# Two long VectorE instructions of a hybrid-block kernel, each in two parts with a recurrence update between

## The chip, the cores and the metric

The kernel runs on one core of one Trainium2 chip. The metric is the device time of one execution in microseconds (us), as the median of the runs. A core has TensorE (PE, with its weight loads as PEld), VectorE (DVE), ScalarE (ACT), GpSimd (POOL) and SyncE (SP, which issues DMAs here). Each works through its own queue of instructions in order; semaphores are all that ties one queue to another.

## The reference

The input x is 8 sequences of 1024 tokens with 256 features. Four layers follow each other, each added to its normalised input: a gated linear attention with its own feed-forward part, a mixture of experts, a recurrence, and the mixture of experts again.

```python
x = x + attn_a(layernorm(x))     # gated linear attention, then h + gelu(ln(h) @ W1 + b1) @ W2 + b2
x = x + ffn(layernorm(x))        # 8 experts, top 2 by softmax of x @ router_w.T
x = x + attn_b(layernorm(x))     # h_t = tanh(x_t @ B + h_(t-1) @ A.T), then hs @ C @ W_out.T + b_out
x = x + ffn(layernorm(x))
```

The recurrence is serial over all 1024 tokens: every step needs the state of the step before. The attention is computed in chunks of 32 tokens: scores of a chunk are multiplied by a causal mask, and a state is carried from chunk to chunk.

## The kernel before, in words

The 1024 tokens are cut into 32 blocks of 32 tokens; a block holds 8 x 32 = 256 rows, two tiles of 128. The work on a block is cut into eight stages, 0 to 7, and the kernel is a software pipeline: iteration `it` works on stage k of block `it - k`. `live(it, k)` is true while that block exists, that is from iteration k to iteration k + 31. There are 39 iterations: 8 written out, a hardware loop over iterations 8 to 31, and 7 written out. In the text a round is one iteration in the loop.

The order inside an iteration is written out by hand for each engine, as one long body. Every engine's body starts at another point of the work, so that iterations of the engines overlap.

The 32 recurrence steps of a block are spread over two iterations (steps 0 to 22 on VectorE as stage 5, steps 23 to 31 as stage 6). A step k is: TensorE `step(k)` (L1135, a 128x8 matmul that waits for `rnn_h`), ScalarE `state_of(k)` (L538 and L539, the same tanh twice, in two roundings), VectorE `split_state(k)` (L773, writes `hs` and raises `rnn_h`). "hs 30" below means the L773 of step 30. Between two steps each engine does pieces of other stages.

Products in full precision are made of three passes over values split in a leading part and a remainder; `rest` (L856) on VectorE computes a remainder. For gelu it reads gT (128x1024) and the leading part gTs[:, 0], both in SBUF, and writes gTs[:, 1]. It stands between hs 29 and hs 30. On TensorE, step 30 is followed by the expert product G2_6, step 31, the value and gate product VG0, the input product of the recurrence (L1406), step 0 of the next block and the attention scores (L1163). The scores write PSUM banks 0 to 3 and so wait, through the list `BANK_ORDER`, for the last readers of these banks; sg0 (L919) is the reader of bank 2. ScalarE goes from `state_of(31)` to kx (four activations), then th and vtok (L562, L563), for which sg0 waits. gTs is read by the product F2, behind the first half of the scores.

The mask (L954) multiplies the scores in four PSUM banks (128x1024) by the causal mask and writes att. It stands between hs 4 and hs 5; dstate (L961) follows hs 5, and it waits for `att` and reads the same banks. xmid (L974), hs 6 and the statistics of xmid come after. By `BANK_ORDER` bank 3 goes from the scores (`SD`, released by `dstate`) to the transposes Y0 of the next iteration, which are the first thing in TensorE's body, behind step 6. ScalarE's body at that point is: the expert norm (L544 with output ym, two activations, which waits for POOL's rstd), `state_of(6)`, the affine on the Y0 bank (L550, twice), `state_of(7)`, the leading parts of T1 and Y0 (L711, L714), `state_of(8)`. VectorE goes from hs 8 through remainders, a combine (L804), a norm (L794), hs 9, the routing, hs 10, the weights of the experts and hs 11 to hs 12.

The bank order and the waits that come of it:

```python
    3: [("Y0", 2, 'hTs'), ("G1_2", 5, ("acc1", 2 * VECTOR_GROUPS, 4)), ("F1A", 4, 'gT'),
            ("G2_3", 7, ("acc2", 2 * VECTOR_GROUPS, 6)), ("TR", 5, 'yrT'), ("SD", 2, 'dstate')],
...
                if live(it, 2):
                    for name, count in readers(it, "Y0"):
                        pe.wait_ge(sem(name), count)
                    pe.wait_ge(sem("y0"), c2)
                    transposed(BANK["Y0"], y0).then_inc(sem("Y0"), 1)
```

Of the kernel before, what the change touches and what calls it, by code (L numbers as in the profile page):

```python
# [6 lines left out]
F32 = mybir.dt.float32  # L7
F32R = mybir.dt.float32r
U32 = mybir.dt.uint32
ALU = mybir.AluOpType  # L10
# [3 lines left out]
P = 128  # L14
B, T, D = 8, 1024, 256
TS = 32
ROUNDS = T // TS
TOK = B * TS
# [5 lines left out]
J = HEADS // HQ  # L24
# [71 lines left out]
def build(nc, x, wts, out):  # L96
    ctx = ExitStack()
    with ctx:
        def sb(name, shape, dt=F32):
            return ctx.enter_context(nc.sbuf_tensor(name, shape, dt))  # L100
# [3 lines left out]
        def sem(name):  # L104
            if name not in sems:
                sems[name] = ctx.enter_context(nc.semaphore(name))
            return sems[name]
# [5 lines left out]
        causal = cst[:, C_CAUSAL:C_CAUSAL + TS]  # L113
# [39 lines left out]
        att = sb("att", [P, J, B, TS])  # L153
# [14 lines left out]
        gT, gTs = sb("gT", [P, FB, TOK]), sb("gTs", [P, 2, FB, TOK], F32R)  # L168
# [42 lines left out]
        ps = ctx.enter_context(nc.psum_tensor("ps", [P, 8, 512], F32))  # L211
        SD = BANK["SD"]
# [30 lines left out]
        def live(it, stage):  # L243

            return not isinstance(it, int) or 0 <= it - stage < ROUNDS

        def cnt(it, stage):

            n = it - stage + 1
            return min(max(n, 0), ROUNDS) if isinstance(it, int) else n  # L250

        def readers(it, use):


            found = {}
            for order in BANK_ORDER.values():
                uses = [u for u, _, _ in order]
                if use in uses:
                    k, at, back = uses.index(use), it, 0
                    while not isinstance(at, int) or at >= 0:  # L260
                        k, at, back = (k - 1, at, back) if k else (len(order) - 1, at - 1, back + 1)
                        _, stage_, reader = order[k]
                        if live(at, stage_):
                            name, count = done_by(reader, cnt(at, stage_))
                            age = (back + stage_, -reader[2] if isinstance(reader, tuple) else 0)
                            if name not in found or age < found[name][0]:
                                found[name] = age, count
                            break
            return [(name, count) for name, (_, count) in found.items()]
# [8 lines left out]
        def past(count):  # L278

            return max(count, 0) if isinstance(count, int) else count  # L280

        def value(eng, count):


            return past(count) if isinstance(count, int) else eng.to_reg(count)
# [447 lines left out]
        def _(dve):  # L733
            v = nc.vector
# [15 lines left out]
            def split_late():  # L750
                dve.wait_ge(sem("weights_lead"), LEAD["late"])
                v.tensor_tensor(wa[:, 1, W_O:W_END], raw(W_O, W_END - W_O), wa[:, 0, W_O:W_END].bitcast(F32), ALU.subtract).then_inc(sem("weights_rest"), 1)
                dve.wait_ge(sem("weights_lead"), LEAD["router"])
                v.tensor_tensor(rws[:, :, 1, :], rw[:], rws[:, :, 0, :].bitcast(F32), ALU.subtract).then_inc(sem("weights_rest"), 1)

            def split_recurrence():
                dve.wait_ge(sem("weights_lead"), LEAD["recurrence_out"])
                dve.wait_ge(sem("a_loaded"), A_LOADED)
                v.tensor_scalar(a_signed, a_lead.bitcast(F32), lead_sign, None, ALU.mult).then_inc(sem("signed"), 1)
                v.tensor_scalar(cw_signed, cw_lead.bitcast(F32), lead_sign, None, ALU.mult).then_inc(sem("signed"), 1)  # L760
                dve.wait_ge(sem("signed"), 2)
                v.tensor_tensor(cw[ROW_REST:ROW_REST + 1, :], bout[ROW_REST:ROW_REST + 1, :], bout_lead.bitcast(F32), ALU.subtract)
                v.scalar_tensor_tensor(aT[0:NB, 0:NB], a_raw, whole_sign, a_signed, ALU.mult, ALU.add)
                v.scalar_tensor_tensor(cw[0:NB, :], ps[0:NB, BANK["RB"], 0:D], whole_sign, cw_signed, ALU.mult, ALU.add).then_inc(sem("weights_rest"), 1)

            def split_state(k, count):

                target = value(dve, (count - 1) * TS + k + 1)
                if k == 0:
                    dve.wait_ge(sem("RO"), past(count - 1))  # L770
                dve.wait_ge(sem("pads_zero"), 1)
                dve.wait_ge(sem("rnn_tanh"), target)
                v.scalar_tensor_tensor(hs[0:NB, :, k], h_whole, keeps_rest, h_lead[:].bitcast(F32), ALU.mult, ALU.subtract).then_inc(sem("rnn_h"), 1)  # L773

            def split_experts(c):
                cols = slice(c * E * D, (c + 1) * E * D)
                dve.wait_ge(sem("weights_lead"), LEAD["experts"])
                v.tensor_tensor(we[:, 1, cols], stage[:, cols], we[:, 0, cols].bitcast(F32), ALU.subtract).then_inc(sem("weights_rest"), 1)
# [18 lines left out]
            def combine(m, k, bank, count):  # L797

                i, pr = k // PAIRS, k % PAIRS
                before = (count - 1) * VECTOR_GROUPS + i * (PAIRS - 1) + pr - 1  # L800
                for e in (2 * pr, 2 * pr + 1):
                    if e > 2:
                        dve.wait_ge(sem(f"acc{m.s}"), past(before * 2 + e % 2))
                    v.scalar_tensor_tensor(m.acc[:, i, :], ps[:, bank, e % 2 * D:(e % 2 + 1) * D], m.coef[:, i, e:e + 1],  # L804
                                                m.acc[:, i, :], ALU.mult, ALU.add).then_inc(sem(f"acc{m.s}"), 1)
# [48 lines left out]
            def rest(parts, whole, name):  # L854

                v.tensor_tensor(parts[:, 1], whole, parts[:, 0].bitcast(F32), ALU.subtract).then_inc(sem(name), 1)  # L856

            def body(it):
                c0, c1, c2, c3, c4, c5, c6, c7 = (cnt(it, k) for k in range(STAGES))
                if live(it, 6):  # L860
# [38 lines left out]
                    split_state(29, c6)  # L899
                if live(it, 4):  # L900
                    dve.wait_ge(sem("gT0"), c4)
                    rest(gTs, gT[:], "gTs")
                if live(it, 6):
                    split_state(30, c6)
                if live(it, 7):
                    dve.wait_ge(sem("acc_start2"), c7 * TILES)
                    dve.wait_ge(sem("moe2"), past((c7 - 1) * GROUPS + 6))
                    combine(m2, 5, BANK["G2_5"], c7)
# [42 lines left out]
                    split_state(4, c5)  # L951
                if live(it, 2):
                    dve.wait_ge(sem("DS1"), c2)
                    v.tensor_tensor(att[:], ps[:, SD:SD + J, 0:TOK].rearrange("p j (b t) -> p j b t", t=TS),  # L954
                                         causal.unsqueeze(1).unsqueeze(1).broadcast_to([P, J, B, TS]), ALU.mult).then_inc(sem("att"), 1)
                if live(it, 5):
                    split_state(5, c5)
                if live(it, 2):
                    dve.wait_ge(sem("att"), c2)
                    dve.wait_ge(sem("state"), past(c2 - 1))  # L960
                    v.tensor_tensor(dstate[:].rearrange("p (i q) c -> p i q c", q=BQ),  # L961
                                         ps[:, SD:SD + BQ, TOK:TOK + TILES * HQ * DV].rearrange("p q (i c) -> p i q c", i=TILES),
                                         blockmask.unsqueeze(1).unsqueeze(1).broadcast_to([P, TILES, BQ, HQ * DV]),
                                         ALU.mult).then_inc(sem("dstate"), 1)
                    if isinstance(it, int) and it == 2:
                        split_late()
                        split_recurrence()
                    if isinstance(it, int) and it == 3:
                        split_experts(0)
                        split_experts(1)  # L970
# [115 lines left out]
                if live(it, 6):  # L1086
                    dve.wait_ge(sem("acc_start2"), past((c6 - 1) * TILES + 1))
                    dve.wait_ge(sem("moe2"), past((c6 - 1) * GROUPS + 2))
                    combine(m2, 1, BANK["G2_1"], c6)

            rounds(dve, body)


# [428 lines left out]
```

## Time and profile before

| | |
|---|---|
| median of 3 runs | 1826.82 us (1826.56 to 1827.68) |
| profiled execution | 1826.96 us |
| its span, first to last instruction | 1825.2 us |
| mean granted TensorE clock | 0.967 |
| TensorE busy | 1678.9 us (92%) |
| VectorE busy | 1370.7 us (75%) |
| ScalarE busy | 1014.0 us (56%) |
| POOL busy | 859.7 us (47%) |
| gTs (L856), 32 instructions | 52.9 us busy |
| att (L954), 32 instructions | 38.6 us busy |
| hs (L773), 1024 instructions | 224.9 us busy |

A timeline row gives the start and the duration in us, the engine, the line, the operation with its output and inputs, their shapes and how many instructions are merged in the row; in brackets at its end stands how long the engine was idle before it and for whom it waited. "Issue" is idle time for which the profile shows no releaser. The ends of matmuls are modelled.

### The profile page before, as it was taken

How to read it: one execution, taken by the hardware profiler on the slowest of the kernel's cores; microseconds unless marked ns; L12 is line 12 of the kernel's file. 1: busy time of each engine (PE TensorE's matmuls, PEld its weight loads, DVE VectorE, ACT ScalarE, POOL GpSimd, SP SyncE). 2: the span in 40 equal slices, each digit the busy share in tenths (PEclk: the TensorE clock that was granted, in tenths of full speed). 3: DMA queues.
4: the chain of work that ended last, by engine and by line, in shares of the span. 5: the costliest groups of instructions: out<-in, count | busy, mean ns of one | idle time of the engine just before them, and what ended most of it. 6: DMA issues, size and time to landing. Idle time of an engine off the chain costs nothing.

```text
span 1825.2 us, 49904 instructions
## 1 busy us (share of the span) xinstructions
PE 1678.9 (92%) x15176; PEld 1409.6 (77%) x15176; DVE 1370.7 (75%) x4878; ACT 1014.0 (56%) x3694; POOL 859.7 (47%) x1293
## 2 busy tenths in 40 slices
PE   5488899999999999999999999999999999998866
PEld 4366788888888888888888888888888888886655
DVE  4466678778888887888888878888878788776544
ACT  4355556656555566565555665655556656554431
POOL 1354445555455455554554555545545555443211
PEclk8699999999999999999999999999999999999878
DMA  4111111100111111001111110011111100110000
GB/s 136 48 30 30 31 36 36 24 25 20 34 34 34 34 34 24 25 20 34 34 34 34 34 23 26 20 34 34 34 34 34 24 25 21 30 31 7 6 6 12
DMA packets 108178, 56.30 MB, mean 31 GB/s; under 512 B 73904, under 2 KB 107344, under 8 KB 107984
## 3 DMA queue, kind: packets, MB, share of 16 engines
q1 hardware_dynamic: 106464, 53.75, 11.5%
q10 hardware_dynamic: 1648, 1.72, 0.3%
q8 instruction: 35, 0.57, 0.1%
q14 instruction: 31, 0.25, 0.0%
HBM read 30.28 MB, written 16.78 MB: 26 GB/s over the span
## 4 chain that ended last, share of the span: by engine, by line
PE 65%; DVE 13%; ACT 8%; issue 7%; POOL 3%; DMA 1%; SPq 1%; DVEq 0%; ACTq 0%; POOLq 0%
PE ps L1118 51%; PE ps L1163 4%; PE ps L1135 3%; PE ps L1124 2%; DVE hs L773 2%; PE ps L1406 1%; ACT ps L550 1%; POOL r L385 1%; ACT ym L544 1%; DVE st L783 1%; DVE oh L847 1%; DVE stage L804 1%; DVE xhat L794 1%; PE ps L1151 1%; DVE y L794 1%
## 5 line engine op out<-in xcount | busy, mean ns | idle before, releaser
L1118 PE MATMUL ps<-we,yT 128*128 128x512 f32 x3072 | 825.5, 412 | 0.0
L1118 PEld LDWEIGHTS ps<-we,yT 128*128 128x128 f32 x3072 | 546.4, 191 | 101.9
L538 ACT ACTIVATE h_lead<-ps 48x8 fp32r<-48x8 f32 x1024 | 173.6, 170 | 628.3 <-PE ps L1135 624.1
L773 DVE SCALAR_TENSOR_TENSOR hs<-ps,cst,h_lead 48x8 fp32r<-48x8 f32 x1024 | 224.9, 220 | 175.9 <-ACT ps L539 164.1
L1135 PEld LDWEIGHTS ps<-hs,aT 128*128 128x128 f32 x1024 | 195.4, 191 | 146.8 <-issue 119.2
L1135 PE MATMUL ps<-hs,aT 128*128 128x8 f32 x1024 | 208.2, 203 | 61.4 <-DVE hs L773 58.2
L413 POOL TENSOR_TENSOR part<-part 128x256 f32<-128x256 f32 x64 | 46.9, 733 | 347.9 <-ACT part L557 347.9
L804 DVE SCALAR_TENSOR_TENSOR stage<-ps,coef,stage 128x256 f32<-128x256 f32 x384 | 184.4, 480 | 34.5 <-PE ps L1118 22.4
L804 DVE SCALAR_TENSOR_TENSOR acc<-ps,coef,acc 128x256 f32<-128x256 f32 x384 | 183.8, 479 | 11.9 <-POOL acc L415 1.7
L435 POOL TENSOR_TENSOR orstd<-omean,mhalf 128x32 f32<-128x32 f32 x32 | 174.0, 5438 | 2.7
L539 ACT ACTIVATE ps<-ps 48x8 f32<-48x8 f32 x1024 | 163.0, 159 | 0.0
L1118 PE MATMUL ps<-h2Ts,wa 128*128 128x256 f32 x768 | 107.5, 290 | 0.0
L1118 PE MATMUL ps<-wa,hTs 128*128 128x512 f32 x384 | 107.5, 416 | 0.0
L1118 PE MATMUL ps<-wa,gTs 128*128 128x256 f32 x768 | 106.3, 287 | 0.0
L413 POOL TENSOR_TENSOR stage<-stage 128x256 f32<-128x256 f32 x64 | 47.0, 735 | 121.8 <-ACT stage L557 121.8
L1118 PEld LDWEIGHTS ps<-h2Ts,wa 128*128 128x128 f32 x768 | 96.4, 191 | 2.9
L1118 PEld LDWEIGHTS ps<-wa,gTs 128*128 128x128 f32 x768 | 94.1, 188 | 1.3
L383 POOL TENSOR_SCALAR r<-mv 128x2 f32<-128x2 f32 x64 | 18.4, 288 | 157.6 <-DVE mv L789 156.4
L1163 PE MATMUL ps<-qt,kx 32*128 32x32 f32 x2048 | 72.9, 281 | 8.7 <-issue 5.8
L1118 PEld LDWEIGHTS ps<-wa,hTs 128*128 128x128 f32 x384 | 69.6, 194 | 11.8
L1163 PEld LDWEIGHTS ps<-qt,kx 32*128 32x128 f32 x2048 | 66.9, 195 | 12.9 <-issue 12.0
L550 ACT ACTIVATE ps<-ps,lnb,lnw 128x256 f32<-128x256 f32 x128 | 62.4, 522 | 19.7 <-PE ps L1124 19.7
(181 smaller groups left out, 3387.7 us busy)
## 6 DMA issues: line engine op xcount, KB each, us to landing
xin<-in_x SPq DMA_DIRECT2D x64, 128.0 KB
vrow<-vtok SPq DMA_DIRECT2D x32, 256.0 KB, 2.2
vx<-vrow SPq DMA_DIRECT2D x128, 64.0 KB, 2.0
sx<-smid SPq DMA_DIRECT2D x128, 64.0 KB
xag<-in_x SPq DMA_DIRECT2D x64, 128.0 KB
out<-stage SPq DMA_DIRECT2D x64, 128.0 KB
stage<-in_experts SPq DMA_DIRECT2D x1, 2048.0 KB, 8.7
stage<-in_Wvg SPq DMA_DIRECT2D x1, 512.0 KB, 5.1
```

Source lines behind the costliest of these rows:

```text
L413: g.tensor_tensor(m.part[:, i, 0, :], m.part[:, i, 0, :], m.part[:, i, 1, :], ALU.add).then_inc(sem(f"part{m.s}"), 1)
L435: g.tensor_tensor(orstd[:], omean[:], mhalf[:], ALU.pow).then_inc(sem("orstd"), 1)
L538: a.activation(h_lead[:], ps[0:NB, BANK["RB"], k * B:(k + 1) * B], ACT.Tanh)
L539: a.activation(h_whole, ps[0:NB, BANK["RB"], k * B:(k + 1) * B], ACT.Tanh).then_inc(sem("rnn_tanh"), 1)
L550: ins = a.activation(ps[:, bank, c * TOK:(c + 1) * TOK], ps[:, bank, c * TOK:(c + 1) * TOK], ACT.Identity, bias=lnb[:, c:c + 1], scale=lnw ...
L773: v.scalar_tensor_tensor(hs[0:NB, :, k], h_whole, keeps_rest, h_lead[:].bitcast(F32), ALU.mult, ALU.subtract).then_inc(sem("rnn_h"), 1)
L794: ins = v.tensor_scalar(dst[:, i, :], src[:, i, :], mean[:, i:i + 1], scale[:, i:i + 1], ALU.subtract, ALU.mult)
L804: v.scalar_tensor_tensor(m.acc[:, i, :], ps[:, bank, e % 2 * D:(e % 2 + 1) * D], m.coef[:, i, e:e + 1], m.acc[:, i, :], ALU.mult, ALU.add) ...
L1118: ins = t.matmul(dst, left(lp, c), right(rp, c), start=(n == 1), stop=(n == 3 * chunks))
L1124: ins = t.transpose(ps[:, dst_bank, c * TOK + i * P:c * TOK + (i + 1) * P], src[:, i, c * P:(c + 1) * P], ident)
L1135: return t.matmul(ps[0:NP, BANK["RB"], k * B:(k + 1) * B], aT[:], hs[:, :, (k - 1) % TS], start=False, stop=True, skip_group_check=True)
L1163: ins = t.matmul(ps[:, SD + j, b * TS:(b + 1) * TS], kx[r, b, :, :].rearrange("p h t -> p (h t)"), qt[r, b * TS:(b + 1) * TS], start=True, ...
```

## The change

The remainder of gelu is computed in two instructions of 128x512, one before hs 30 and one after it; the semaphore `gTs` is raised by the second. The mask over the scores is done in two instructions, each over two of the four banks, one before hs 5 and one after it; `att` is raised by the second, and dstate follows it directly. Nothing else changes: no operation, buffer or wait is added to another engine.

```diff
--- before.py
+++ after.py
@@ -855,6 +855,15 @@
 
                 v.tensor_tensor(parts[:, 1], whole, parts[:, 0].bitcast(F32), ALU.subtract).then_inc(sem(name), 1)
 
+            def rest_of_gelu(f):
+
+                return v.tensor_tensor(gTs[:, 1, f:f + 2], gT[:, f:f + 2], gTs[:, 0, f:f + 2].bitcast(F32), ALU.subtract)
+
+            def mask_scores(j):
+
+                return v.tensor_tensor(att[:, j:j + 2], ps[:, SD + j:SD + j + 2, 0:TOK].rearrange("p j (b t) -> p j b t", t=TS),
+                                       causal.unsqueeze(1).unsqueeze(1).broadcast_to([P, 2, B, TS]), ALU.mult)
+
             def body(it):
                 c0, c1, c2, c3, c4, c5, c6, c7 = (cnt(it, k) for k in range(STAGES))
                 if live(it, 6):
@@ -899,9 +908,11 @@
                     split_state(29, c6)
                 if live(it, 4):
                     dve.wait_ge(sem("gT0"), c4)
-                    rest(gTs, gT[:], "gTs")
+                    rest_of_gelu(0)
                 if live(it, 6):
                     split_state(30, c6)
+                if live(it, 4):
+                    rest_of_gelu(2).then_inc(sem("gTs"), 1)
                 if live(it, 7):
                     dve.wait_ge(sem("acc_start2"), c7 * TILES)
                     dve.wait_ge(sem("moe2"), past((c7 - 1) * GROUPS + 6))
@@ -951,11 +962,11 @@
                     split_state(4, c5)
                 if live(it, 2):
                     dve.wait_ge(sem("DS1"), c2)
-                    v.tensor_tensor(att[:], ps[:, SD:SD + J, 0:TOK].rearrange("p j (b t) -> p j b t", t=TS),
-                                         causal.unsqueeze(1).unsqueeze(1).broadcast_to([P, J, B, TS]), ALU.mult).then_inc(sem("att"), 1)
+                    mask_scores(0)
                 if live(it, 5):
                     split_state(5, c5)
                 if live(it, 2):
+                    mask_scores(2).then_inc(sem("att"), 1)
                     dve.wait_ge(sem("att"), c2)
                     dve.wait_ge(sem("state"), past(c2 - 1))
                     v.tensor_tensor(dstate[:].rearrange("p (i q) c -> p i q c", q=BQ),
```

## Rows read from the trace of the kernel before

**Rows 1.** Busy time by stretch: length, PE PEld DVE ACT POOL, clock, DMA share, GB/s.

```profile
712.18:764.29 52.11, 51.02 (x477) 42.98 (x476) 42.26 (x153) 31.06 (x115) 26.96 (x41) 1.00 0.12 30
```

**Rows 2.** Waits of TensorE, whole span: total us, times, longest.

```profile
PE ps L1135 <- DVE hs L773: 58.2, 110, 1.4
...
PE ps L1124 <- DVE dstate L961: 4.7, 5, 2.0
```

**Rows 3.** Chain that ended last, one round: start us, us, what.

```profile
722.88 0.05 PE ps L1135
...
727.73 0.97 ACT ps L550 x2
...
730.09 0.11 DVE hs L773
...
738.12 0.24 PE ps L1135
```

**Rows 4.** Gelu's remainder, all rounds: duration ns min/median/max.

```profile
L856 DVE TENSOR_TENSOR gTs<-gT,gTs x32: 1206/1665/2247, 100.7 to 1699.3; 128x1024 fp32r<-128x1024 f32 x32
```

**Rows 5.** Timeline around gelu's remainder: start us, us, engine line; [idle before].

```profile
712.18 1.67 DVE L856 TENSOR_TENSOR gTs<-gT,gTs 128x1024 fp32r<-128x1024 f32 x1
...
712.51 1.64 PE L1118 MATMUL ps<-we,yT 128*128 128x512 f32 x6
...
712.71 2.28 POOL L465 TENSOR_TENSOR res<-res,xmid 128x512 f32<-128x512 f32 x1
712.76 0.16 ACT L539 ACTIVATE ps<-ps 48x8 f32<-48x8 f32 x1
...
713.77 0.22 DVE L773 SCALAR_TENSOR_TENSOR hs<-ps,cst,h_lead 48x8 fp32r<-48x8 f32 x1
...
714.10 0.19 PEld L1135 LDWEIGHTS ps<-hs,aT 128*128 128x128 f32 x1 [0.39 <-issue]
714.13 0.24 PE L1135 MATMUL ps<-hs,aT 128*128 128x8 f32 x1
...
714.24 1.67 PE L1118 MATMUL ps<-wa,hTs 128*128 128x512 f32 x6
```

**Rows 6.** Timeline, same round, up to the scores.

```profile
714.41 0.17 ACT L538 ACTIVATE h_lead<-ps 48x8 fp32r<-48x8 f32 x1 [0.37 <-PE ps L1135]
...
716.81 0.42 DVE L919 SCALAR_TENSOR_TENSOR sg<-th,ps 128x256 f32<-128x256 f32 x1 [0.52 <-ACT vtok L563]
...
717.41 1.01 PEld L1163 LDWEIGHTS ps<-qt,kx 32*128 32x128 f32 x32 [0.27 <-issue]
```

**Rows 7.** Timeline, same round, around the mask over the scores.

```profile
723.73 0.74 DVE L783 BATCH_NORM_STATS2 st<-mx_in 128x6 f32<-128x256 f32 x2
...
724.57 0.25 DVE L789 BATCH_NORM_AGGREGATE mv<-st 128x2 f32<-128x6 f32 x2
...
724.91 1.20 DVE L954 TENSOR_TENSOR att<-ps,cst 128x1024 f32<-128x1024 f32 x1
...
725.29 1.64 PE L1118 MATMUL ps<-we,yT 128*128 128x512 f32 x6
...
725.57 0.16 ACT L539 ACTIVATE ps<-ps 48x8 f32<-48x8 f32 x1
...
726.04 0.22 DVE L773 SCALAR_TENSOR_TENSOR hs<-ps,cst,h_lead 48x8 fp32r<-48x8 f32 x1
726.17 0.67 DVE L961 TENSOR_TENSOR dstate<-ps,cst 128x512 f32<-128x512 f32 x1
...
726.76 0.17 PE L1135 MATMUL ps<-hs,aT 128*128 128x8 f32 x1
...
726.99 0.65 PE L1124 MATMUL ps<-cst,y 128*128 128x128 f32 x4
...
727.67 0.16 ACT L539 ACTIVATE ps<-ps 48x8 f32<-48x8 f32 x1
...
727.93 0.22 DVE L773 SCALAR_TENSOR_TENSOR hs<-ps,cst,h_lead 48x8 fp32r<-48x8 f32 x1 [0.48 <-ACT ps L539]
```

## The prediction

> **What bounds the kernel now.** I read the page first, for the busy shares (in the table above): TensorE leads, with VectorE not far behind. The busy times of one steady round (gelu's remainder to gelu's remainder) sharpen that: 52.11 us, of them TensorE 51.02 and VectorE 42.26, at the full granted clock [rows 1]. The waits of TensorE name VectorE's recurrence update hs as what it stood for longest, 58.2 us in 110 places, and show five waits for dstate [rows 2]. The chain of waits over one round then tells the two regimes. From 738.12 on it stays on TensorE until 722.88 + 52.11 of the round after. Between 722.9 and 738.1 it leaves TensorE: through the statistics of mx_in and the expert norm on ScalarE to the affine after the Y0 transposes (ACT ps L550), by ScalarE in order to a recurrence tanh and VectorE's hs (730.09), and through VectorE's full queue back to the recurrence matmul at 738.12 [rows 3]. In stretch A (TensorE) a saved TensorE wait counts in full; in stretch B a delay of a link counts in full once its slack is used. The change touches one place in each.
>
> **Gelu's remainder (stretch A).** Now gTs starts at 712.18 and the next hs (step 30) at 713.77, though its tanh began at 712.76 [rows 5]. A tanh releases hs some 0.26 us after its start where VectorE is free (727.67 to 727.93 [rows 7]), so hs could have gone at 713.02. TensorE shows the price: its expert product begins at 712.51 and the recurrence matmul behind it at 714.13, 1.62 us later, its weight load idle for 0.39 [rows 5]; the same product without that wait takes 1.47 (725.29 to 726.76 [rows 7]). The matmul is also 0.24 long after the wait and 0.17 without [rows 5, 7], so it would end at 713.98 + 0.17 = 714.15 instead of 714.37: 0.22 earlier. The profile hides this wait inside the modelled end of the product, which is why the kernel looks busy there.
>
> The first half's length is not in the trace. Whole remainders take 1.21 at least, 1.67 in the middle and 2.25 at most [rows 4]; half of the shortest is 0.6, and half of it with all the 0.46 of delay added is 1.07. So the first half ends at 712.8 to 713.25, hs runs at 713.02 to 713.25, is done by 713.47, and its reader sees it 0.11 later (713.99 to the load at 714.10 [rows 5]). With a load of 0.19 that is 713.77, before the matmul's undisturbed 713.98: the wait goes at either end. The second half then ends between 713.9 and 714.3 against 713.85; what is queued behind it is the combine of two 0.5 us and hs 31, whose readers on TensorE come after a 1.5 us product: hidden.
>
> What is late next? The scores. Their first load is idle for 0.27 until 717.41, just behind sg (716.81 + 0.42), which waited 0.52 for ScalarE's vtok; ScalarE runs through from the tanh at 714.41, which waited for our recurrence matmul [rows 6]. So the scores move with that tanh, by 0.22 less the rounding of a busy ScalarE: I take **0.20 us per round** gained (bounds 0, if the POOL operation beside it, res at 712.71 for 2.28, stretches both halves; and 0.26: product to product is 1.73 [rows 5], less the undisturbed 1.47). 30 of the 39 iterations have gelu's remainder and a step 30 together: **-6.0 us**. Gelu's product reads gTs four microseconds later: no cost.
>
> **The mask over the scores (stretch B).** Now the mask att starts at 724.91, hs 5 at 726.04, dstate at 726.17 [rows 7]. A 128x512 operation from PSUM holds the queue for 0.60 (dstate is 0.67 long, and a successor starts 0.07 before an end, as hs 5 at 726.04 behind the mask's 726.11), so two halves cost 1.20 against 1.13: 0.07 for the extra instruction. The larger part is order. The first half is over at 725.51. The tanh of step 5 began at 725.57 and releases hs at 725.83. VectorE now stands 0.32 with the second half behind that wait; before, the mask's other half filled the time. hs 725.83, second half 725.96 to 726.63. Then dstate waits for the completion of att, which it could ignore before because hs 5 lay between: 0.10 as the reader of the statistics does (723.73 + 0.74, reader at 724.57 [rows 7]), nothing at the least; I take 0.07. So dstate starts at 726.70 (726.63 to 726.73) and ends at 727.37, 0.53 later than now.
>
> Who waits for dstate? The code makes the Y0 transposes of the next iteration wait for it, as they reuse the scores' bank. They start at 726.99, 0.15 after dstate's end, and last 0.65 [rows 7]; the waits of TensorE name dstate in five other places [rows 2]. Some of that 0.15 may be slack (a loop branch), or all latency, so they move to 727.43 to 727.52 and end at 728.08 to 728.17. ScalarE's affine takes up its work some 0.04 later. It is now at 727.73, without idle time behind a tanh at 727.67 [rows 3, 7], and would start at 728.12 to 728.21: 0.39 to 0.48 late. I take **0.45**. From there ScalarE works in order to the tanh that releases hs at 730.09, then VectorE in order to 738.12, where TensorE already waits [rows 3]: nothing to absorb it. What hs 5 gains (0.2) is worth nothing, because step 6 stands behind the product of 725.29 until 726.76, well after even the old hs [rows 7]. xmid, behind dstate, slips by 0.53 into the 0.48 idle before hs 6 [rows 7]: about even. The mask and hs 5 meet, with a Y0 to follow, in 28 iterations: **+12.6 us**. Bounds: 0 (if the tanh came early) and dstate's own 0.56 without any slack, 15.7 us.
>
> **Sum.** -6.0 + 12.6 = +6.6 us. The profiled execution took 1826.96 with a span of 1825.2, 1.76 around it, and agrees with the median of 1826.82 to 0.14: 1833.4 us.
>
> **A rule weighed.** TensorE does stand behind a long VectorE instruction in stretch A [rows 5]. The Trainium skill, Perfetto Trace Analysis, section Optimizing Scalar/DVE Operations, says that where VectorE is not saturated but makes bubbles on other engines, breaking up instructions may let work finish sooner. By that rule both splits should help or be harmless, the sum would be -6, and it is a rival below. The row speaks for it at gelu and against it at the mask, where the split puts a wait where none was.
>
> **The rivals.**
> 1. Faster: the cover holds at the mask. If hs 5 were ready by 725.51, when the first half is over, dstate would slip only by 0.07 and 0.10, which the 0.15 ahead of the transposes takes up; the gelu gain stands alone: -6.0, 1820.8 us. For it: the plain wait of TensorE at step 31. Against it: the tanh begins at 725.57, after that point, because the matmul of step 5 is held by TensorE's own order. It decides from 0.32 us of earlier tanh. Chance 0.12. The rule of the Trainium skill weighed above (Perfetto Trace Analysis, Optimizing Scalar/DVE Operations) would come out here.
> 2. No change beyond measurement: the delay at Y0 is real but partly absorbed (an affine later by 0.2 to 0.3, or gain 0.26 with loss 0.36): 0 to +3.6, about 1828.5. For it: the 0.15 ahead of the transposes and the 0.09 from their end (727.64) to the affine, gaps that may be slack. Against: a chain without idle time behind it [rows 3]. Chance 0.20.
> 3. Slower by more: the gelu halves collide with POOL's res and the gain fails, the mask costs 0.45: +12.6, 1839.4. Against: hs 30 has 0.2 to spare at the worst. Chance 0.10.
> That the change doesn't do what it says can be left out: the order on VectorE is written out by hand.
>
> **How the numbers follow.** Forecast 0.58, rivals 0.12, 0.20, 0.10. Time 1833.4. The likeliest case alone spans 1830.5 to 1838. The range reaches into rivals 2 and 3: 1824 to 1840. About 0.2% (3.7 us) can be told from no change: slower 0.58 + 0.10 = 0.68, same 0.20, faster 0.12.
>
> **What would show it.** In the steady rounds: 64 gTs instructions of 0.7 to 0.9 us, the load of step 31 with little idle time left before it (now 0.39); 64 att of 0.67, idle time of about 0.3 before hs 5 put down to ScalarE's tanh; dstate starting 0.8 behind hs 5 instead of 0.13; an affine (L550) with some 0.4 idle, put down to the transposes; a round of 52.36 us instead of 52.11. I am wrong if the affine still follows its tanh without idle time, or if the round is shorter than before.

## The result and the profile after

| | before | changed |
|---|---|---|
| median | 1826.69 us (4 runs, 1825.57 to 1827.68) | 1859.44 us (4 runs, 1854.58 to 1859.88) |
| ratio | | 1.0173, 95% interval 1.0156 to 1.0191 |
| span of the profiled execution | 1825.2 us | 1857.9 us |

Slower, as forecast, but by 32.7 us and not by 6.6; the time lies outside the range of 1824 to 1840. The runs of this kernel differ by some us among themselves: before ran from 1824.6 to 1838.1 us in all the comparisons below, with mean granted clocks of 0.958 to 0.967.

The head of the page, and its group for gelu's remainder (line, engine, operation, output and inputs, shapes, count, busy us, mean ns, idle before):

```profile
span 1857.9 us, 49968 instructions
...
PE 1681.5 (91%) x15176; PEld 1408.8 (76%) x15176; DVE 1404.5 (76%) x4942; ACT 1014.6 (55%) x3694; POOL 856.5 (46%) x1293
...
L860 DVE TENSOR_TENSOR gTs<-gT,gTs 128x512 fp32r<-128x512 f32 x64 | 85.2, 1333 | 0.0
```

VectorE is 34 us busier. Nearly all of it is in this group: the halves of gelu's remainder are busy for 85.2 us, the whole ones were for 52.9. Half a remainder takes 1333 ns on average, so the two together take 2.7 us where the whole one had a median of 1665 ns [rows 4]: 1.0 us more a round.

One steady round, from gelu's remainder to gelu's remainder, against [rows 1]: 53.10 us instead of 52.11, TensorE as busy as before (50.99), VectorE 1.1 us busier.

```profile
725.69:778.79 53.10, 50.99 (x477) 42.80 (x476) 43.39 (x156) 31.08 (x115) 26.86 (x41) 1.00 0.12 30
```

What TensorE waits for in 24 rounds of the loop (line waited for, total us, times, longest us):

```profile
PE ps L1146 <- DVE hs L773: 23.3, 72, 0.4
PE ps L1135 <- DVE dstate L972: 13.6, 24, 0.6
PE ps L1417 <- DVE hs L773: 10.6, 24, 0.5
```

The lines have moved by the edit: L1146 is the recurrence matmul (L1135 before), L1135 the transposes (L1124 before). Before, the same view over 24 rounds had this, and no wait for dstate:

```profile
PE ps L1135 <- DVE hs L773: 14.0, 48, 0.3
```

Three waits are new, each once a round. The Y0 transposes stand for dstate (0.57 us each). The recurrence matmul of step 8 stands for hs 7 (0.41), which makes 72 waits out of 48. The input product of the recurrence (L1417, L1406 before) stands for hs 31 (0.44). The first is the one that the prediction named, and the second follows from it. The third it had called hidden.

**Gelu's remainder after the change**, the stretch of [rows 5] (start us, duration us, engine, line):

```profile
724.99 1.27 POOL L462 TENSOR_TENSOR state<-smid,dstate 128x512 f32<-128x512 f32 x1
...
725.69 1.12 DVE L860 TENSOR_TENSOR gTs<-gT,gTs 128x512 fp32r<-128x512 f32 x1
...
726.02 1.64 PE L1129 MATMUL ps<-we,yT 128*128 128x512 f32 x6
...
726.22 1.75 POOL L465 TENSOR_TENSOR res<-res,xmid 128x512 f32<-128x512 f32 x1
726.27 0.16 ACT L539 ACTIVATE ps<-ps 48x8 f32<-48x8 f32 x1
...
726.73 0.22 DVE L773 SCALAR_TENSOR_TENSOR hs<-ps,cst,h_lead 48x8 fp32r<-48x8 f32 x1
726.87 1.65 DVE L860 TENSOR_TENSOR gTs<-gT,gTs 128x512 fp32r<-128x512 f32 x1
727.26 0.19 PEld L1146 LDWEIGHTS ps<-hs,aT 128*128 128x128 f32 x1
727.50 0.17 PE L1146 MATMUL ps<-hs,aT 128*128 128x8 f32 x1
...
727.91 0.66 POOL L468 TENSOR_TENSOR elast<-eq,one 128x8 f32<-128x8 f32 x1
728.44 0.99 DVE L804 SCALAR_TENSOR_TENSOR stage<-ps,coef,stage 128x256 f32<-128x256 f32 x2
...
729.34 0.21 DVE L773 SCALAR_TENSOR_TENSOR hs<-ps,cst,h_lead 48x8 fp32r<-48x8 f32 x1
...
729.61 1.13 PE L1417 MATMUL ps<-stage,bin_ 128*128 128x256 f32 x4 [0.44 <-DVE hs L773]
...
731.47 1.09 PE L1174 MATMUL ps<-qt,kx 32*128 32x32 f32 x32
```

The last row is the scores. Before, they were here, in the clock of [rows 5]:

```profile
717.44 1.09 PE L1163 MATMUL ps<-qt,kx 32*128 32x32 f32 x32 [0.20 <-issue]
```

Read POOL and VectorE together. POOL's state update (L462) ends at 726.26, and the first half, begun at 725.69, ends 0.55 after that, at 726.81. POOL's res takes 1.75 and, if its own work is the 1.28 of other 128x512 additions, works from 726.69 to 727.97. The second half, begun at 726.87, ends 0.55 after that, at 728.52, and POOL's elast, an instruction of 0.2, starts at 727.91 and lasts until 728.57. So these durations fit two engines that take turns here: an instruction that meets the other engine's is drawn out until the other is over. In all 24 rounds of the loop each half ends 0.54 to 0.56 after the end of the POOL instruction ahead of it. The recurrence part went as forecast (hs at 726.73, the load of step 31 without idle time, its matmul 1.48 behind the product's start instead of 1.62), but the combine starts at 728.44 and hs 31 at 729.34, both 1.0 later behind the start of the remainder than before, and TensorE stands 0.44 at L1417. The scores start 5.78 behind the start of the remainder (731.47 and 725.69), where it was 5.26 (717.44 and 712.18): 0.52 us lost a round.

**The mask after the change**, the stretch of [rows 7]:

```profile
737.01 0.69 DVE L955 TENSOR_TENSOR mx_in<-ps,res 128x512 f32<-128x512 f32 x1 [0.38 <-PE ps L1129]
...
738.94 0.67 DVE L864 TENSOR_TENSOR att<-ps,cst 128x512 f32<-128x512 f32 x1
...
739.59 0.16 ACT L539 ACTIVATE ps<-ps 48x8 f32<-48x8 f32 x1
739.85 0.23 DVE L773 SCALAR_TENSOR_TENSOR hs<-ps,cst,h_lead 48x8 fp32r<-48x8 f32 x1 [0.24 <-ACT ps L539]
740.00 0.67 DVE L864 TENSOR_TENSOR att<-ps,cst 128x512 f32<-128x512 f32 x1
...
740.70 0.69 DVE L972 TENSOR_TENSOR dstate<-ps,cst 128x512 f32<-128x512 f32 x1
...
741.53 0.65 PE L1135 MATMUL ps<-cst,y 128*128 128x128 f32 x4 [0.57 <-DVE dstate L972]
...
742.22 0.99 ACT L550 ACTIVATE ps<-ps,lnb,lnw 128x256 f32<-128x256 f32 x2 [0.36 <-PE ps L1135]
...
743.82 0.24 PE L1146 MATMUL ps<-hs,aT 128*128 128x8 f32 x1 [0.41 <-DVE hs L773]
```

Second half, dstate, transposes and affine follow each other closely (0.03, 0.14 and 0.04 us between them), and the recurrence matmul of step 8 then stands 0.41 for hs 7; dstate ends 4.38 us behind the start of mx_in (737.01), where it was 3.85 before (722.99 and 726.84).

### The profile page after: what moved, and what is told of

Read it like the earlier page. It is cut to its first block, busy times and chain, and to the rows that moved or that the text cites. A ratio compares the mean times of both kernels' runs of the same rounds, so it can differ in the third digit from the quotient of the medians.

```text
span 1857.9 us, 49968 instructions
## 1 busy us (share of the span) xinstructions
PE 1681.5 (91%) x15176; PEld 1408.8 (76%) x15176; DVE 1404.5 (76%) x4942; ACT 1014.6 (55%) x3694; POOL 856.5 (46%) x1293
## 4 chain that ended last, share of the span: by engine, by line
PE 63%; DVE 19%; issue 8%; ACT 6%; DMA 1%; POOL 1%; SPq 1%; DVEq 1%; ACTq 0%; POOLq 0%
PE ps L1129 50%; DVE gTs L860 4%; PE ps L1174 4%; PE ps L1146 3%; DVE stage L804 3%; DVE hs L773 2%; PE ps L1135 2%; DVE oh L847 1%; ACT h_lead L538 1%; DVE att L864 1%; PE ps L1183 1%; DVE dstate L972 1%; ACT ps L550 1%; PE ps L1162 1%; DVE xhat L794 1%
## 5 line engine op out<-in xcount | busy, mean ns | idle before, releaser
L1146 PEld LDWEIGHTS ps<-hs,aT 128*128 128x128 f32 x1024 | 196.7, 192 | 146.4 <-issue 122.5
L1146 PE MATMUL ps<-hs,aT 128*128 128x8 f32 x1024 | 208.5, 204 | 68.4 <-DVE hs L773 67.3
L413 POOL TENSOR_TENSOR part<-part 128x256 f32<-128x256 f32 x64 | 46.7, 730 | 358.7 <-ACT part L557 358.7
L413 POOL TENSOR_TENSOR stage<-stage 128x256 f32<-128x256 f32 x64 | 47.0, 734 | 119.7 <-ACT stage L557 119.7
L860 DVE TENSOR_TENSOR gTs<-gT,gTs 128x512 fp32r<-128x512 f32 x64 | 85.2, 1333 | 0.0
```

The costliest lines, as they stand in the source:

```text
L413: g.tensor_tensor(m.part[:, i, 0, :], m.part[:, i, 0, :], m.part[:, i, 1, :], ALU.add).then_inc(sem(f"part{m.s}"), 1)
L860: return v.tensor_tensor(gTs[:, 1, f:f + 2], gT[:, f:f + 2], gTs[:, 0, f:f + 2].bitcast(F32), ALU.subtract)
L1146: return t.matmul(ps[0:NP, BANK["RB"], k * B:(k + 1) * B], aT[:], hs[:, :, (k - 1) % TS], start=False, stop=True, skip_group_check=True)
```

## The experiments

The comparison of the experiments is best made round by round, as the loop runs at the full granted clock (1.00 in the stretches shown below), while the iterations written out ahead of it (the fill) and behind it (the drain) do not. The table gives medians over 21 rounds of the loop, each worked out from the starts of three instructions: mx_in (L944 in the numbering of before), the recurrence matmul of step 13 (738.12 in [rows 3]) and gelu's remainder.

| kernel | round | mx_in to step 13 | step 13 to remainder | remainder to mx_in | parts of the remainder | median us | ratio, 95% interval |
|---|---|---|---|---|---|---|---|
| before | 52.13 | 15.14 | 26.18 | 10.81 | 1.67 | | |
| changed | 53.09 | 15.58 | 26.17 | 11.34 | 1.12, 1.64 | 1859.44 | 1.0173 (1.0156 to 1.0191) |
| gelu_only | 52.65 | 15.14 | 26.17 | 11.34 | 1.13, 1.64 | 1843.64 | 1.0081 (1.0056 to 1.0106) |
| mask_only | 52.58 | 15.59 | 26.18 | 10.81 | 1.67 | 1840.70 | 1.0054 (1.0029 to 1.0079) |
| gelu_res_late | 51.93 | 15.13 | 26.18 | 10.62 | 1.13, 0.67 | 1822.90 | 0.9962 (0.9944 to 0.9980) |
| gelu_early | 52.11 | 15.13 | 21.91 | 15.07 | 1.21 | 1829.12 | 0.9998 (0.9981 to 1.0015) |
| mask_adjacent | 52.13 | 15.14 | 26.19 | 10.80 | 1.67 | 1826.67 | 0.9995 (0.9985 to 1.0005) |
| gelu_adjacent | 53.29 | 15.14 | 26.18 | 11.97 | 2.83 in all | 1861.41 | 1.0174 (1.0149 to 1.0199) |
| res_late | 52.12 | 15.13 | 26.18 | 10.80 | 1.66 | 1826.30 | 1.0004 (0.9985 to 1.0022) |
| both_res_late | 52.39 | 15.58 | 26.19 | 10.62 | 1.12, 0.67 | 1842.07 | 1.0068 (1.0043 to 1.0093) |
| whole_free | 51.95 | 15.14 | 26.18 | 10.62 | 1.21 | 1825.36 | 0.9986 (0.9969 to 1.0002) |
| split_free | 51.94 | 15.14 | 26.18 | 10.62 | 0.67, 0.67 | 1823.97 | 0.9963 (0.9946 to 0.9980) |

The first four experiments ran beside 24 runs of before (median 1828.39, 1825.91 to 1838.14), the next four beside 19 (1826.67), the last two beside 16 (1827.4). The ratios are on record with the runs and aren't the quotients of these medians (for both_res_late the quotient is 1.0084), so differences of a few us are read from the rounds.

**gelu_only**: the change without its mask part.

```diff
                     dve.wait_ge(sem("gT0"), c4)
-                    rest(gTs, gT[:], "gTs")
+                    rest_of_gelu(0)
                 if live(it, 6):
                     split_state(30, c6)
+                if live(it, 4):
+                    rest_of_gelu(2).then_inc(sem("gTs"), 1)
```

> Only gelu's remainder is in two parts, the mask is whole. Theory 1 (lock): a VectorE instruction with two SBUF inputs and a POOL instruction never run together; the second part stands behind POOL's res and the stretch from gelu's remainder to mx_in stays 0.5 us longer, as in the changed kernel (11.3 instead of 10.8), the stretch behind mx_in is that of before (15.1). Round 52.65, total 1826.8 + 30 x 0.53 = about 1843. Theory 2 (the two changes only hurt together, the gelu split alone gains the 0.2 that was forecast): 1821.

Measured: 1843.64 us, the round 52.65, 0.52 longer, all of it between remainder and mx_in (0.53). This is theory 1.

**mask_only**: the change without its gelu part.

```diff
-                    v.tensor_tensor(att[:], ps[:, SD:SD + J, 0:TOK]..., causal..., ALU.mult).then_inc(sem("att"), 1)
+                    mask_scores(0)
                 if live(it, 5):
                     split_state(5, c5)
                 if live(it, 2):
+                    mask_scores(2).then_inc(sem("att"), 1)
```

> Only the mask is in two parts. Theory 1: the loss is in the stretch from mx_in to the recurrence matmul of step 13, 0.45 us a round through dstate, the Y0 transposes and the affine; 28 rounds, 12.6 us, total 1839.4, round 52.56. Rival: with the gelu part out, TensorE reaches this stretch earlier and some of the 0.45 is slack: 1830 or less.

Measured: 1840.70 us, the round 0.45 longer, all of it between mx_in and step 13. The two parts add exactly: 52.13 + 0.52 + 0.45 = 53.10 against 53.09.

**gelu_res_late**: gelu_only, and POOL's res (L465) is moved behind smid.

```diff
-                if live(it, 3):
-                    pool.wait_ge(sem("res"), c3)
-                    g.tensor_tensor(res[:], res[:], xmid[:], ALU.add).then_inc(sem("res_mid"), 1)
...
                     g.tensor_tensor(smid[:], state[:], dec[:]..., ALU.mult).then_inc(sem("smid"), 1)
+                if live(it, 3):
+                    pool.wait_ge(sem("res"), c3)
+                    g.tensor_tensor(res[:], res[:], xmid[:], ALU.add).then_inc(sem("res_mid"), 1)
```

> Gelu's remainder in two parts, mask whole, and POOL's addition of xmid to res is moved behind the product smid, where VectorE has no instruction with two SBUF inputs. Theory 1 (lock): the first part still waits for POOL's state update (about 1.1 us), the second finds no POOL operation and takes 0.67; hs 31 is on time, TensorE's wait at step 31 is gone, total 1826.8 - 6 = 1821. Theory 3 (a half of gelu's remainder is slow in itself, by its shape or its place in memory): the second part stays at 1.65, total about 1843.

Measured: 1822.90 us, ratio 0.9962 (0.9944 to 0.9980), faster than both kernels. Its timeline around the remainder:

```profile
714.18 1.28 POOL L462 TENSOR_TENSOR state<-smid,dstate 128x512 f32<-128x512 f32 x1
...
714.90 1.12 DVE L860 TENSOR_TENSOR gTs<-gT,gTs 128x512 fp32r<-128x512 f32 x1
...
715.41 0.17 ACT L538 ACTIVATE h_lead<-ps 48x8 fp32r<-48x8 f32 x1 [0.77 <-PE ps L1146]
...
715.94 0.22 DVE L773 SCALAR_TENSOR_TENSOR hs<-ps,cst,h_lead 48x8 fp32r<-48x8 f32 x1
716.07 0.67 DVE L860 TENSOR_TENSOR gTs<-gT,gTs 128x512 fp32r<-128x512 f32 x1
716.16 0.64 POOL L383 TENSOR_SCALAR ra<-mv_a 128x2 f32<-128x2 f32 x1
```

The same half that took 1.65 beside res takes 0.67 here: its length was not its own. POOL's elast (a row not shown) and the first small ra instruction are stretched to 0.66 and 0.64 in its place, and the profile shows no other engine waiting for them. The remainder-to-mx_in stretch is 10.62, 0.19 shorter than before; the prediction's term for gelu was 0.20.

**gelu_early**: both long instructions whole, the remainder moved on VectorE from behind hs 29 to behind hs 26.

```diff
                 if live(it, 6):
                     split_state(26, c6)
+                if live(it, 4):
+                    dve.wait_ge(sem("gT0"), c4)
+                    rest(gTs, gT[:], "gTs")
...
                     split_state(29, c6)
-                if live(it, 4):
-                    dve.wait_ge(sem("gT0"), c4)
-                    rest(gTs, gT[:], "gTs")
```

> Gelu's remainder whole, mask whole, and the remainder stands behind hs 26 instead of behind hs 29, where POOL is idle in the trace of before for 0.7 us more. Theory 1 (lock): the remainder takes 1.21 instead of 1.67, POOL's next operation (part) starts up to 0.6 late, hs 30 goes 0.26 us behind its tanh, the load of step 31 has no idle time left, 0.20 to 0.24 us a round are gained: about 1820.5. Theory 3 (1.67 is its own duration): it stays at 1.67, hs 27 comes late and the gain is lost: 1826 to 1830.

Measured: the remainder takes 1.21, as theory 1 has it, and the round stays at 52.11: the gain that was expected did not come. The timeline shows where it went:

```profile
713.45 1.21 DVE L856 TENSOR_TENSOR gTs<-gT,gTs 128x1024 fp32r<-128x1024 f32 x1
...
714.10 1.17 POOL L413 TENSOR_TENSOR stage<-stage 128x256 f32<-128x256 f32 x1 [2.09 <-ACT stage L557]
...
716.03 1.29 POOL L452 TENSOR_TENSOR og<-onorm,sg 128x512 f32<-128x512 f32 x1
...
717.43 0.42 DVE L900 SCALAR_TENSOR_TENSOR sg<-th,ps 128x256 f32<-128x256 f32 x1 [1.13 <-POOL og L452]
...
717.77 0.22 DVE L773 SCALAR_TENSOR_TENSOR hs<-ps,cst,h_lead 48x8 fp32r<-48x8 f32 x1
718.10 0.19 PEld L1135 LDWEIGHTS ps<-hs,aT 128*128 128x128 f32 x1 [0.23 <-issue]
...
718.75 0.23 DVE L773 SCALAR_TENSOR_TENSOR hs<-ps,cst,h_lead 48x8 fp32r<-48x8 f32 x1 [0.76 <-ACT ps L539]
```

Now the remainder, there first, holds POOL up: the sum part (L413) takes 1.17 instead of 0.74, and og comes about 0.4 later for it. VectorE's sg waits 1.13 for og (0.74 before) with hs 29 behind it, and the load of step 30 is idle for 0.23. Hs 30 follows its tanh by 0.26, as meant; TensorE has lost the same 0.2 one step earlier. The exclusion works in both directions: here POOL is the one that is held up.

**mask_adjacent**: the two parts of the mask follow each other, hs 5 behind both.

```diff
+                    mask_scores(0)
+                    mask_scores(2).then_inc(sem("att"), 1)
                 if live(it, 5):
                     split_state(5, c5)
```

> The mask is in two parts with nothing between them, hs 5 behind both as before; gelu whole. It parts the 0.45 us a round of the mask. Theory 1: the loss is the order (VectorE stands for the tanh of step 5 with half a mask left, and dstate waits for the mask's own completion), the second instruction itself costs 0.07: dstate 0.07 later, the round 52.13 to 52.2, total within 2 us of before. Rival (two 128x512 instructions cost more than one of 128x1024, whatever stands between): round 52.4 and more.

Measured: 1826.67 us against 1826.67, the round 52.13. The two halves together take 1.27 us (725.44 to 726.71 in its trace) where the whole mask took 1.20, and dstate ends 0.06 later, but the affine starts 4.75 behind mx_in against 4.74 before: the slack behind dstate takes it up. The second instruction costs nothing that arrives at a round; the loss of the mask part is what stands between its halves.

**gelu_adjacent**: the two parts of the remainder follow each other, hs 30 behind both.

```diff
+                    rest_of_gelu(0)
+                    rest_of_gelu(2).then_inc(sem("gTs"), 1)
                 if live(it, 6):
                     split_state(30, c6)
```

> Gelu's remainder is in two parts with nothing between them, hs 30 behind both; mask whole. Theory 1 says that POOL and such a VectorE instruction exclude each other, and this shows who comes first when POOL's res already waits. (a) VectorE's second part follows at once: parts of 1.12 and 0.67, hs 30 is 0.07 later, round 52.2. (b) POOL's res goes between: parts of 1.12 and about 1.8, hs 30 and step 31 are 1.2 later, round 53.3, about 1862. Theory 3 (halves slow in themselves): 1.12 and 1.65, round 53.2.

Measured: 1861.41 us, round 53.29, case (b):

```profile
722.03 2.83 DVE L860 TENSOR_TENSOR gTs<-gT,gTs 128x512 fp32r<-128x512 f32 x2
...
722.57 1.73 POOL L465 TENSOR_TENSOR res<-res,xmid 128x512 f32<-128x512 f32 x1
...
724.78 0.21 DVE L773 SCALAR_TENSOR_TENSOR hs<-ps,cst,h_lead 48x8 fp32r<-48x8 f32 x1
...
725.14 0.24 PE L1145 MATMUL ps<-hs,aT 128*128 128x8 f32 x1 [1.13 <-DVE hs L773]
```

Both halves with nothing between them take 2.83, the whole instruction 1.67. In the seam POOL's res, which had begun at 722.57, went first: VectorE ends 0.56 behind res (724.86 and 724.30), and TensorE stood 1.13 at step 31. So what one instruction buys here is that POOL can't come between; the recurrence update has no part in this loss.

**res_late**: the kernel before with res behind smid (the edit on POOL as above, nothing else).

> The kernel before with POOL's res moved behind smid, both long VectorE instructions whole: the control for the version with the move and the gelu split. Theory 1: gelu's remainder still waits for POOL's state update and takes 1.67, hs 30 is as late as before, the round stays 52.13 and the time that of before. Rival (the 0.2 us a round came from the move and not from the split): round 51.93, 5 us faster.

Measured: 1826.30 us, ratio 1.0004 (0.9985 to 1.0022), round 52.12, the remainder 1.66. The move alone does nothing: the whole remainder still waits for the state update ahead of res.

**both_res_late**: the changed kernel with res behind smid (the same edit on POOL).

> The changed kernel (both splits) with POOL's res moved behind smid. Theory 1: the stretches add: -0.20 for gelu, +0.45 for the mask, round 52.38, about 7 us over before; of the changed kernel's loss, 20 us go. Rival (the loss of gelu's part in the changed kernel has another cause than res): round 52.9 or more.

Measured: the round is 52.39, as forecast; the time is 1842.07 us, 15.4 over before instead of 7. The stretches of its profiled execution (length, busy PE, PEld, DVE, ACT, POOL, granted clock, DMA share, GB/s), up to the first mx_in of the loop, over 24 rounds, and from there to the end:

```profile
0.00:311.89 311.89, 241.72 (x2437) 203.94 (x2440) 194.79 (x600) 160.54 (x471) 134.63 (x214) 0.87 0.17 47
311.89:1569.03 1257.14, 1215.00 (x11405) 1028.98 (x11392) 1019.62 (x3696) 746.51 (x2761) 644.87 (x961) 1.00 0.12 30
1569.03:1841.70 272.67, 221.66 (x1392) 182.71 (x1375) 164.25 (x646) 107.96 (x464) 76.51 (x120) 0.88 0.05 13
```

The 24 rounds are 6.2 us longer than before's 1250.91 (below), 24 x 0.26. The other 10 us lie in the fill and the drain, where this execution had mean clocks of 0.87 and 0.88 against 0.90 and 0.89 before. Part of the excess goes with the clock of these runs: three of the four had mean clocks of 0.959 and 0.960 and took 1840.64 to 1843.67, where a run of before at 0.960 took 1832.41; the fourth, at 0.964, took 1838.05, where before took 1826.19 to 1826.67. Compared so, 8 to 12 us are left against the 7 of the forecast. What the rest is, is not settled.

**whole_free** and **split_free**: POOL's state update is moved behind inner_rstd (POOL's chain of small instructions on ra, 128x2 each), and res behind smid as above; the remainder is whole in the first, in two parts around hs 30 in the second. The mask is whole.

```diff
-                if live(it, 2):
-                    pool.wait_ge(sem("smid"), c2)
-                    pool.wait_ge(sem("dstate"), c2)
-                    g.tensor_tensor(state[:], smid[:], dstate[:], ALU.add).then_inc(sem("state"), 1)
...
                     inner_rstd(c0)
+                if live(it, 2):
+                    pool.wait_ge(sem("smid"), c2)
+                    pool.wait_ge(sem("dstate"), c2)
+                    g.tensor_tensor(state[:], smid[:], dstate[:], ALU.add).then_inc(sem("state"), 1)
```

> Both long VectorE instructions whole, as before; POOL's state update and res both moved behind the chain of inner_rstd, so that only POOL's instructions of 128x2 and 128x8 are beside gelu's remainder. Theory 1 (lock): the whole remainder takes 1.21 to 1.4 instead of 1.67, hs 30 runs 0.3 to 0.45 earlier, its reader sees it before TensorE has finished the product, and step 31 comes 0.1 to 0.2 us earlier: round 51.93 to 52.05, 2 to 5 us under before without any split. Theory 3 (1.67 is the instruction's own length beside a busy ScalarE or for other reasons): 1.67 and 52.13.

> Gelu's remainder in two parts, mask whole, POOL's state update and res moved as in the kernel beside it. Theory 1: both parts take 0.67 to 0.85, hs 30 goes 0.26 behind its tanh, 0.4 earlier than with res alone moved, but step 31 then waits for TensorE's own product, so the round stays at the 51.93 of the version with res alone moved (at best 51.87): about 1821 to 1823. Rival (hs 30 still bounds step 31 there): 51.7 or less.

Measured: the whole remainder takes 1.21 in nearly all rounds, against a median of 1.665 in [rows 4] (duration ns min/median/max):

```profile
L856 DVE TENSOR_TENSOR gTs<-gT,gTs x32: 1206/1207/2251, 100.0 to 1698.8; 128x1024 fp32r<-128x1024 f32 x32
```

POOL pays in its place: its L385 (128x2), 0.71 us in before, begins with the remainder at 714.31 and takes 1.77. The round is 51.95, with no split at all. Over the whole kernel its median is 1825.36 and its ratio 0.9986 (0.9969 to 1.0002) isn't told from no change. The split version comes to 51.94 and 1823.97, 0.9963 (0.9946 to 0.9980). In both, and in gelu_res_late, the gain stops at 0.19 a round: step 31 then stands behind TensorE's own product (its matmul starts 1.47 to 1.48 behind the product's start in all three), so an earlier hs 30 buys nothing more.

## Why the prediction was wrong

**Which step failed.** The term for gelu's remainder, -0.20 us a round, measured at +0.52 with the mask left out (gelu_only), outside its bounds of 0 and a gain of 0.26. Inside it, one step failed, the bound on the halves' length: "half of it with all the 0.46 of delay added is 1.07 ... The second half then ends between 713.9 and 714.3 against 713.85 ... hidden." The first half came out near that bound, 1.12 (0.67 of its own and 0.45 of delay). The second took 1.65 and ended 2.83 us after the start of the first; in the clock of before that is 715.0. I had taken 0.46 as the whole delay that POOL can cause, spread over the work. It was what was left of one POOL instruction, the state update, and the second half met the next one, res, for another 0.98. All that I called hidden then was late: the combine, hs 31, and TensorE behind it.

**It stood in the rows.** [rows 5] has POOL's res at 712.71 for 2.28. The state update, with the same shape, takes 1.28 in before, just ahead of it. Res ended at 714.99, 1.28 after 713.71: if its own work is as long, it began 0.14 before gelu's remainder (712.18 + 1.67 = 713.85) ended; res and elast do the same in the changed kernel, 0.12 and 0.15 before the end of the halves they wait for. I used this row for a rival ("the gelu halves collide with POOL's res and the gain fails") and gave it +12.6, a gelu term of 0, at 0.10. The right question of that row was what the 1.0 us of its stretch is, and on which engine it lands if VectorE lets go in the middle: by the rows of the changed kernel POOL's res is over 0.5 sooner, and VectorE pays 1.0.

**A page states it.** The Trainium skill, SBUF — State Buffer, section "SBUF: two separate sides", says that VectorE and GpSimd share a pair of SBUF ports which is an exclusive lock for a whole instruction, taken by whichever starts first: a VectorE instruction in a two-port mode or, against a GpSimd instruction that reads SBUF, with two SBUF inputs, or one of GpSimd; the loser blocks fully. The traces here agree: 1.65 beside res, 0.67 without it, for the same half. They show the durations and not the ports, so that the lock is what makes the engines take turns is the page's statement. By these durations one sentence ahead of the prediction is too strong: semaphores are not all that ties one engine's queue to another's. Here VectorE and POOL also hold each other up with no semaphore between them. The other rule, that of the Trainium skill, Perfetto Trace Analysis, section Optimizing Scalar/DVE Operations, on breaking up instructions, which the prediction weighed, came true for the gelu split only where POOL's res was out of the way (0.9962), and brought a loss at the mask, where VectorE had made no bubble.

**What was right.** The gain at step 31: once POOL is out of the way it is 0.19 to 0.20 a round (gelu_res_late, 51.93). The mask, step by step: the tanh releases hs 5 at 739.85, 0.26 behind its start; second half 0.15 later; dstate 0.53 late, transposes 0.14 behind its end; the affine idle for 0.36 on the transposes and 0.47 late against mx_in (5.21 us behind it, 4.74 before), and nearly nothing behind it absorbs it: 0.45 a round against a forecast of 0.45. Rivals 1 and 2 fall with mask_only. The 0.07 that the split itself was charged shows on VectorE alone and is absorbed (mask_adjacent). The idle time ahead of hs 5 was 0.24, not 0.3: the profile counts it from the first half's end, 0.67 behind its start, and the prediction had counted from 0.60. That the kernel got slower as forecast is right by this term alone; the sign of gelu's was wrong.

**The sum.** The stretches of before and of the changed kernel, cut at the same instructions:

```profile
0.00:305.85 305.85, 236.77 (x2437) 198.14 (x2440) 192.64 (x589) 160.53 (x471) 135.66 (x214) 0.90 0.18 48
305.85:1556.76 1250.91, 1224.72 (x11406) 1031.38 (x11391) 1013.84 (x3649) 745.88 (x2761) 647.12 (x961) 1.00 0.12 30
1556.76:1825.20 268.44, 217.36 (x1392) 180.12 (x1373) 164.18 (x641) 107.57 (x464) 76.89 (x120) 0.89 0.05 14
```

```profile
0.00:312.23 312.23, 239.51 (x2438) 201.07 (x2440) 197.08 (x601) 160.36 (x471) 135.42 (x214) 0.88 0.18 48
312.23:1586.26 1274.03, 1223.15 (x11406) 1027.62 (x11391) 1040.88 (x3697) 746.15 (x2761) 644.84 (x961) 1.00 0.12 30
1586.26:1857.90 271.64, 218.84 (x1392) 180.10 (x1375) 166.57 (x646) 108.06 (x464) 76.21 (x120) 0.89 0.05 13
```

The 24 rounds hold 23.1 of the 32.7 us (24 x 0.96). The fill is 6.4 longer and the drain 3.2. Some of that is the same two losses in the written-out iterations; some goes with the clock (0.88 against 0.90 in the fill), which differs between executions: gelu_early, whose rounds are no longer than those of before, had a fill of 311.59 us at a mean clock of 0.88. The forecast's counts of 30 and 28 iterations with +0.53 and +0.45 would give 28.5; the other 4 us are not taken apart.

## What to carry to other kernels

Before cutting a VectorE instruction that reads two SBUF tensors, look at what POOL does beside it: a long one keeps POOL out once, two let a POOL instruction in between, and the second half pays for it (gelu_adjacent). Row by row, an instruction that is longer than others of its shape is the sign, on either engine, and moving the neighbour can give the gain without the cut. And an update put between two halves helps only if it is ready when the first half ends, and if the half that now comes last has no one waiting for it.

## What was not expected of the hardware

VectorE's 128x512 instruction with two SBUF inputs takes 0.67 alone, and 1.12 or 1.65 in the changed kernel, where one of POOL's 128x512 additions is under way as it starts. In both cases it ends 0.55 after POOL's end. This does not hold for every POOL instruction as the profile draws it: in split_free the second half started while POOL's L385 (128x2) was recorded for 0.26 us more, and still took 0.67. With two such VectorE instructions back to back, POOL's waiting instruction goes between them (2.83 for both). The halves of the mask around hs 5 and dstate, which read one operand from PSUM, keep 0.67 to 0.69 in every kernel here; dstate had 0.69 with POOL's res<-xag beside it (740.57 to 741.85 in the changed kernel), which kept its 1.28. This compares different instructions; no run changes only where one operand lies.
